# A graph-attention layer on one core: the keys' stage with its work on x spread per tile

## The chip, the cores and the metric

The kernel runs on one core of one Trainium2 chip. The metric is the device time of one execution in microseconds. Before the change the median of 3 runs is 2405.26 us (2391.13 to 2406.40).

## The reference, cut to what matters

x has 6250 rows (nodes) of 256 features; there are 206,250 edges. The part that the change touches is the layer norm and the keys of the linear attention:

```
xn   = layernorm(x)                                  # per row, eps 1e-5
k    = elu(xn @ Wk.T) + 1
ksum = k.sum(rows);  context = k.T @ v   per head    # v = xn @ Wv.T
x1   = x + gnn(xn) + attention(xn)                   # gnn sums (1+eps)*xn and xn[src] by dst
out  = x1 + lstm_ffn(layernorm(x1))
```

The kernel never forms v here: it sums M = xn.T @ k over all rows and multiplies by Wv later. It also keeps xn twice: split into a high part (low 12 mantissa bits cut away) and a low part, both in SBUF as the operand of the later edge sums, and scaled by 1 + eps in DRAM.

## The kernel before, in words

Rows are handled in 49 tiles of 128 (NT), grouped into ten chunks of five (XT = 5, XCH = 10). Each engine has its own hand-written order, and engines meet at semaphores. Chunks of x are loaded by SyncE into a ring of four buffers, `x_ring` (L289). The keys' stage is one loop over the tiles on each engine:

- TensorE (L512 to L554), iteration i: two transposes of tile i (L519), the two key products of tile i-1 (L529, four MATMUL records a tile, as fp32 takes two passes), then the product M of tile i-2 (L536), which needs k_s of that tile.
- ScalarE (L880 to L911), iteration i: copy of the transposed tile to xnT (L886), exp of k_e of tile i-1 (L890). Beside these, once in five tiles: the square root for the row statistics of the chunk two ahead (L871; it needs another activation table than exp, so each one brings two table loads), the high half of a chunk (L900), the chunk scaled by 1 + eps into `row_out` (L906), and the store of `row_out` to DRAM (L910). Before L906 writes the one buffer `row_out`, ScalarE waits for the store of the chunk before (`row_in`); there the store was issued four tiles earlier.
- VectorE (L1303 to L1347), iteration i: k_s = max(k, 0) + exp of tile i-1 (L1310), min(k, 0) of tile i (L1314). Beside these, once in five tiles: `row_stats` of chunk q+2 (L1156, L1160) at tile 0 of a chunk, `row_cut` (L1179) at tile 1, `row_norm` of chunk q+2 (L1166, L1169) at tile 2. At fixed tiles (3, 4, 6, 8, 9, 13, 18, 24, 28, 29, 33) it also does steps on the edge list, L1204 to L1292, some of 2 to 5 us.
- GpSimd (L435 to L452): the low half of a chunk, x minus the cut x (L445), then for each of its tiles k_acc += k_s (L452).

k_e, k_s and the PSUM bank of the keys are double buffered (t % 2, banks 4 and 5). Ahead of the loop VectorE does statistics and normalisation of chunks 0 and 1 and then clears PSUM bank 6 (L1299), which releases TensorE. After the stage follow the queries (from L564), the edge sums (L637), the second norm and the LSTM.

Of the kernel before, what the change touches and what calls it, by code (L numbers as in the profile page):

```python
# [45 lines left out]
CB = (0, 1, 2, 7)  # L46
MAGIC = float(3 * 2 ** 22)
# [16 lines left out]
def build(nc, a, out):  # L64
# [8 lines left out]
    with ExitStack() as ctx:  # L73
# [106 lines left out]
        k_e = [scr[:, v * D:(v + 1) * D] for v in range(2)]  # L180
        k_s = [scr[:, 512 + v * D:512 + (v + 1) * D] for v in range(2)]
        k_acc = scr[:, 1024:1024 + D]
# [103 lines left out]
        def _(sp):  # L286
# [24 lines left out]
            for q in range(XCH - XR):  # L311
                sp.wait_ge(S["m_mm"], XT * (q + 1))
                sp.wait_ge(S["lo_q"], q + 1)
                sp.wait_ge(S["row_act"], q + 1)
                load_x(q + XR)
# [3 lines left out]
            sp.wait_ge(S["lo_q"], XCH - 2)  # L319
# [4 lines left out]
            sp.wait_ge(S["lo_q"], XCH)  # L324
# [89 lines left out]
        def _(pool):  # L414
# [20 lines left out]
            for q in range(XCH):  # L435
                pool.wait_ge(S["cut_v"], q + 1)
                if q == 2:
                    pool.wait_ge(S["key_ok"], 2)
                    pool.dma_start(key_d, key_all).then_inc(S["key_st"], 16)
                if q == XCH // 2:  # L440
                    pool.wait_ge(S["hist_ps"], 2)
                if q == KEY_CH:
                    pool.wait_ge(S["key_st"], 16)
                h = len(tiles(q))
                pool.tensor_tensor(xhl[:, q * XT:q * XT + h, 1, :], x_ring[q % XR][:, 0:h, :], x_cut.bitcast(F32)[:, 0:h, :],  # L445
                                   ALU.subtract).then_inc(S["lo_q"], 1)
                for t in tiles(q):
                    pool.wait_ge(S["k_v"], t + 1)
                    if t:
                        pool.wait_ge(S["acc_q"], t)  # L450
                    r = rows_of(t)
                    pool.tensor_tensor(k_acc[0:r, :], k_acc[0:r, :], k_s[t % 2][0:r, :], ALU.add).then_inc(S["acc_q"], 1)  # L452
# [46 lines left out]
        def _(pe):  # L499
# [12 lines left out]
            for i in range(NT + 2):  # L512
                if i < NT:
                    t = i
                    pe.wait_ge(S["xn_ok"], t // XT + 1)
# [5 lines left out]
                if 1 <= i <= NT:  # L521
# [4 lines left out]
                    if t >= 2:  # L526
                        pe.wait_ge(S["k_v"], t - 1)
                    for c in range(2):
                        last = mm(psum[0:rows_of(t), 4 + t % 2, 0:D], xnT[:, c, t * P:t * P + rows_of(t)], wkv[:, c, :],  # L529
                                  start=(c == 0), stop=(c == 1))  # L530
                    last.then_inc(S["k_ps"], 1)
                if i >= 2:
                    t = i - 2
                    pe.wait_ge(S["k_v"], t + 1)
                    for c in range(2):
                        last = mm(psum[:, 6, c * D:(c + 1) * D], xr(t)[0:rows_of(t), c * P:(c + 1) * P], k_s[t % 2][0:rows_of(t), :],  # L536
# [324 lines left out]
        def _(act):  # L861
# [13 lines left out]
            row_std(1)  # L875
# [4 lines left out]
            for i in range(NT + 1):  # L880
# [6 lines left out]
                if i >= 1:  # L887
                    t = i - 1
                    act.wait_ge(S["k_min"], t + 1)
                    fn(k_e[t % 2], k_e[t % 2], ACT.Exp).then_inc(S["k_exp"], 1)  # L890
                if i < NT:
                    if i % XT == 0 and q + 2 < XCH:
                        row_std(q + 2)
                    if i % XT == 2:
                        act.wait_ge(S["cut_v"], q + 1)
                        if q == XCH // 2:
                            act.wait_ge(S["hist_ps"], 2)
                        if q == KEY_CH:
                            act.wait_ge(S["key_st"], 16)
                        fn(xhl[:, q * XT:q * XT + len(tiles(q)), 0, :], x_cut.bitcast(F32)[:, 0:len(tiles(q)), :], ACT.Copy).then_inc(S["hi_act"], 1)  # L900
                    if i == tiles(q)[-1]:
                        if q == 0:
                            act.wait_ge(S["eps1_v"], 1)
                        if q:
                            act.wait_ge(S["row_in"], 16 * q)
                        fn(row_out[:, 0:len(tiles(q)), :], x_ring[q % XR][:, 0:len(tiles(q)), :], ACT.Copy, scale=eps1).then_inc(S["row_act"], 1)  # L906
                if i and (i % XT == 0 or i == NT):
                    q = (i - 1) // XT
                    act.wait_ge(S["row_act"], q + 1)
                    act.dma_start(row_d[(q * XT + 1) * P:(tiles(q)[-1] + 2) * P, :].rearrange("(t p) d -> p t d", p=P),  # L910
                                  row_out[:, 0:len(tiles(q)), :]).then_inc(S["row_in"], 16)  # L911

            act.wait_ge(S["lo_q"], XCH)
# [224 lines left out]
        def _(dve):  # L1138
# [14 lines left out]
            def row_stats(q):  # L1153
                dve.wait_ge(ld_x[q % XR], 16 * (q // XR + 1) + (16 if q == XCH - 1 else 0))
                for t in range(len(tiles(q))):
                    last = dve.bn_stats(stats[:, 6 * t:6 * t + 6], x_ring[q % XR][:, t, :])  # L1156
                last.then_inc(S["ln_v"], 1)
                dve.wait_ge(S["ln_v"], 2 * q + 1)
                for t in range(len(tiles(q))):
                    last = dve.bn_aggr(mv[q % 2][:, 2 * t:2 * t + 2], stats[:, 6 * t:6 * t + 6])  # L1160
                last.then_inc(S["ln_v"], 1)
                dve.wait_ge(S["ln_v"], 2 * q + 2)

            def row_norm(q):
# [535 lines left out]
```

## Time and profile before

| | us |
|---|---|
| median of 3 runs | 2405.26 |
| lowest, highest | 2391.13, 2406.40 |
| the profiled execution | 2404.46 |
| its span in the profile | 2402.6 |
| keys' stage: first transpose (L519) to the end of the last M product (L536) | 23.5 to 211.6 |
| granted TensorE clock, mean of the span | 0.957 |

Rows of the timeline give start, duration, engine, line, operation and tiles; the bracket is the idle time of that engine just before it, and what ended it. L12 is line 12. PEld is the weight load of TensorE. A granted clock of 1.00 is 2.4 GHz, 0.50 is 1.2 GHz. Tile numbers: `scr` holds k_e, k_s, k_acc and x_cut; `halves` is the split x; `rs_buf` holds `row_out` and one ring buffer, `wx` the other three.

### The profile page before, as it was taken

What the parts mean: (1) busy time and instruction counts of PE and PEld (TensorE: products, weight loads), DVE (VectorE), ACT (ScalarE), POOL (GpSimd) and SP (SyncE); (2) the same over time, 40 slices, a digit from 0 to 9 for tenths busy, and PEclk for the clock granted to TensorE, in tenths of its full rate; (3) what the DMA queues carried; (4) which work ended last, traced back from release to release, by engine and by line L of the source; (5) the groups of instructions that cost most, each with busy time, mean ns of one, the idle gap of its engine ahead of it and who ended that gap; (6) DMA issues with size and microseconds to landing.
All of it is one profiled execution on the core that took longest, in us unless ns stands there. A gap on an engine that the chain in (4) does not pass through costs nothing.

```text
span 2402.6 us, 46078 instructions
## 1 busy us (share of the span) xinstructions
PE 2094.8 (87%) x14220; PEld 1687.2 (70%) x14220; DVE 1617.1 (67%) x4262; ACT 1177.4 (49%) x3155; POOL 160.3 (7%) x185
## 2 busy tenths in 40 slices
PE   4678989999999999999899899988888888888734
PEld 3457876666666666666687788878877887888623
DVE  6756888777777777777277677755565565655684
ACT  2354435555555555555232566655554554555615
POOL 3233001000000000000000000000000000000060
PEclk9789998999999999999999999999999999999975
DMA  4222220010010110100332122233333332334103
GB/s 111 72 75 70 95 96 26 26 31 24 29 31 24 31 31 22 31 28 26 110 97 65 52 119 103 119 103 118 112 94 102 113 117 85 111 111 119 60 7 100
DMA packets 100568, 173.79 MB, mean 72 GB/s; under 512 B 7901, under 2 KB 74779, under 8 KB 100221
## 3 DMA queue, kind: packets, MB, share of 16 engines
q1 hardware_dynamic: 70538, 86.80, 11.3%
q10 hardware_dynamic: 28240, 81.21, 10.9%
q0 software_dynamic: 1744, 5.21, 0.7%
q8 instruction: 24, 0.39, 0.1%
q14 instruction: 22, 0.18, 0.0%
HBM read 114.63 MB, written 58.56 MB: 72 GB/s over the span
## 4 chain that ended last, share of the span: by engine, by line
PE 51%; DVE 18%; ACT 9%; issue 8%; ACTq 2%; DMA 2%; DVEq 1%; POOL 0%; SPq 0%; POOLq 0%
PE psum L626 25%; PE psum L779 8%; PE psum L621 7%; PE psum L736 4%; DVE scr L1579 3%; DVE scr L1577 3%; ACT scr L1047 2%; ACT scr L1055 2%; DVE scr L1575 2%; DMA out_dram<-wq 2%; DVE scr L1371 2%; DVE bufB L1497 1%; DVE bufB L1581 1%; ACTq L1066 1%; ACT scr L1014 1%
## 5 line engine op out<-in xcount | busy, mean ns | idle before, releaser
L626 PE MATMUL psum<-halves,counts 128*128 128x512 f32 x2401 | 759.8, 423 | 16.2 <-ACT counts L952 16.2
L1396 DVE TENSOR_TENSOR wx<-rs_buf 128x392 bf16<-128x392 bf16 (+1 forms) x1568 | 545.0, 390 | 212.2 <-PE psum L621 208.4
L779 PE MATMUL psum<-bufB,wx 128*128 x4800 | 602.0, 282 | 81.8 <-DVE bufB L1581 72.8
L779 PEld LDWEIGHTS psum<-bufB,wx 128*128 128x128 f32 x4800 | 563.7, 193 | 120.0 <-issue 109.1
L952 ACT ACTIVATE counts<-psum 128x392 fp32r<-128x392 f32 x784 | 390.3, 498 | 359.1 <-PE psum L621 357.7
L626 PEld LDWEIGHTS psum<-halves,counts 128*128 128x128 f32 x2401 | 393.7, 189 | 65.9 <-ACT counts L952 21.8
L621 PEld LDWEIGHTS psum<-wx 128*128 128x128 bf16 x3136 | 170.8, 99 | 199.0 <-issue 192.0
L621 PE MATMUL psum<-wx 128*128 128x98 bf16 x3136 | 284.8, 213 | 4.0 <-DVE wx L1396 2.9
L1581 DVE TENSOR_TENSOR bufB<-scr 128x125 f32 (+1 forms) x300 | 87.1, 290 | 146.6 <-ACT scr L1055 146.6
L736 PE MATMUL psum<-bufA,wx 128*128 (+1 forms) x800 | 180.1, 376 | 3.1 <-POOL rs_buf L487 3.1
L1055 ACT ACTIVATE scr<-scr 128x125 f32<-128x125 f32 x300 | 92.2, 307 | 172.1 <-DVE scr L1579 172.1
L736 PEld LDWEIGHTS psum<-bufA,wx 128*128 128x128 f32 x800 | 146.7, 188 | 20.1 <-issue 3.3
L1575 DVE TENSOR_TENSOR scr<-scr 128x125 f32<-128x125 f32 x300 | 85.7, 286 | 106.8 <-ACT scr L1047 106.8
L1014 ACT ACTIVATE scr<-psum,bias_c 128x125 f32<-128x125 f32 x400 | 107.9, 382 | 64.0 <-PE psum L746 63.9
L1042 ACT ACTIVATE psum<-bufA 128x500 f32<-128x500 f32 x144 | 85.7, 595 | 102.1 <-ACT scr L1055 102.1
L1047 ACT ACTIVATE scr<-psum 128x250 f32<-128x250 f32 x300 | 110.2, 367 | 31.8 <-PE psum L779 31.8
L1569 DVE COPY psum<-bufA 128x500 f32<-128x500 f32 x144 | 97.7, 678 | 15.1 <-issue 15.0
L493 POOL TENSOR_TENSOR bufC<-bufC,bufB 128x250 f32<-128x250 f32 x50 | 40.7, 857 | 945.2 <-ACT bufB L1111 945.2
L1497 DVE TENSOR_SCALAR bufB<-psum,bias_c 128x250 f32<-128x250 f32 x192 | 89.0, 474 | 18.0 <-PE psum L736 16.6
L1579 DVE TENSOR_TENSOR scr<-scr 128x125 f32<-128x125 f32 x300 | 87.0, 290 | 10.4
L1577 DVE TENSOR_TENSOR scr<-scr 128x125 f32<-128x125 f32 x300 | 84.8, 283 | 0.0
L1051 ACT ACTIVATE scr<-psum 128x125 f32<-128x125 f32 x300 | 83.4, 278 | 0.0
(249 smaller groups left out, 2232.9 us busy)
## 6 DMA issues: line engine op xcount, KB each, us to landing
bufA<-gates_of_x ACTq DMA_DIRECT2D x144, 500.0 KB, 3.4
gates_of_x<-bufB SPq DMA_DIRECT2D x24, 1000.0 KB, 3.9
x_times_eps_plus_sums<-scr SPq DMA_DIRECT2D x50, 128.0 KB, 1.7
sums_by_feature<-scr SPq DMA_DIRECT2D x50, 128.0 KB, 1.9
scr<-x_times_eps_plus_sums SPq DMA_DIRECT2D x49, 128.0 KB, 2.0
wx<-in_x_dram SPq DMA_DIRECT2D x25, 250.0 KB
x_plus_mix<-wx SPq DMA_DIRECT2D x25, 250.0 KB, 4.7
bufB<-x_plus_mix SPq DMA_DIRECT2D x25, 250.0 KB, 2.7
```

Of the source, the lines that this page charges most:

```text
L621: last = mm(psum[:, CB[u % 4], g * KEYS:(g + 1) * KEYS], oh_l[r][:, g // 2, :, g % 2], oh_m[r][:, g // 2, :, g % 2], start=True, stop=True)
L626: return mm(psum[:, 3 + v, :], cnt[v][:, hi, :], xhl[:, hi, :, :].rearrange("p s d -> p (s d)"), start=(hi == 0), stop=(hi == NT - 1))
L736: last = mm(psum[:, 4 * v + g, c0 * HC:(c0 + 1) * HC].rearrange("p (s j) -> p s j", s=2), wihv[:, k, m * P:(m + 1) * P], ls_in[:, ds(2 * p ...
L779: return mm(gate_half(u, m, gate), whhv[:, k, (2 * gate + m) * P:(2 * gate + m + 1) * P], h, start=False, stop=(k == 1), skip_group_check= ...
L952: fn(cnt[v][:, :, c * u:c * (u + 1)], psum[:, CB[u % 4], 0:PER * KEYS].rearrange("p (c h) -> p h c", h=NT), ACT.Copy).then_inc(S["c_sb"], 1)
L1014: last = fn(to[:, c * CH:(c + 1) * CH], psum[:, 4 * v + g, c * HC + s * CH:c * HC + (s + 1) * CH], function, bias=bias_c[:, 2 * g + c:2 * ...
L1047: fn(half(s_if, m), psum[:, 4 * u + 2 + m, 0:HC].rearrange("p (g j) -> p g j", g=2), ACT.Sigmoid).then_inc(S["hif_act"], 1)
L1055: fn(th[:, m * CH:(m + 1) * CH], tg_c[1 - u][:, 1, m * CH:(m + 1) * CH], ACT.Tanh).then_inc(S["hth_act"], 1)
L1396: last = tt(to, tab2[:, 0:k_, :].unsqueeze(1).broadcast_to([P, PER // 2, k_, 2]), keysT[v][:, part_, g0:g0 + PER // 2, :].unsqueeze(2).bro ...
L1575: tt(prod[:, 1, cut], s_if[:, 1, cut], tg_c[u][:, 1, cut], ALU.mult)
L1577: tt(prod[:, 0, cut], s_if[:, 0, cut], tg_c[u][:, 0, cut], ALU.mult).then_inc(S["prod_v"], 1)
L1579: tt(tg_c[1 - u][:, 1, cut], prod[:, 0, cut], prod[:, 1, cut], ALU.add).then_inc(S["hc_v"], 1)
```

## The change

The work on x is done per tile. ScalarE's iteration i now does, after exp of tile i-1: the high half of that tile, the scaled row copy of that tile, and after the last tile of a chunk the store; the square root of the next chunk follows at the second tile of each chunk. GpSimd does the low half of one tile and then its k_acc step. VectorE cuts one tile per iteration, takes statistics of one tile per iteration of the chunk after the next (the five aggregations together at its end), and normalises the next chunk in its iterations 2, 3 and 4 (two, two and one tile). Ahead of the loop only chunk 0 is done; the statistics of chunk 1 are done inside iteration 0, after `small_vectors`, which moved there from iteration 3. k_e, k_s and the PSUM bank become three each (banks 4, 5, 7), and TensorE's M product lags by three tiles. `row_out` remains one buffer; its wait now stands at the first tile of each chunk, one tile after the store of the chunk before.

```diff
+KB = (4, 5, 7)
-        k_e = [scr[:, v * D:(v + 1) * D] for v in range(2)]
+        k_e = [scr[:, v * D:(v + 1) * D] for v in range(3)]
...
@@ GpSimd @@
-                pool.tensor_tensor(xhl[:, q * XT:q * XT + h, 1, :], x_ring[q % XR][:, 0:h, :], x_cut.bitcast(F32)[:, 0:h, :],
+                pool.tensor_tensor(xhl[:, t, 1, :], x_ring[q % XR][:, j, :], x_cut.bitcast(F32)[:, j, :],
                                    ALU.subtract).then_inc(S["lo_q"], 1)
...
@@ TensorE @@
-                    if t >= 2:
-                        pe.wait_ge(S["k_v"], t - 1)
+                    if t >= 3:
+                        pe.wait_ge(S["k_v"], t - 2)
...
-                if i >= 2:
-                    t = i - 2
+                if i >= 3:
+                    t = i - 3
                     pe.wait_ge(S["k_v"], t + 1)
...
@@ ScalarE @@
             row_std(0)
-            row_std(1)
...
+                    fn(k_e[t % 3], k_e[t % 3], ACT.Exp).then_inc(S["k_exp"], 1)
+                    q, j = t // XT, t % XT
+                    act.wait_ge(S["cut_v"], t + 1)
...
+                    fn(xhl[:, t, 0, :], x_cut.bitcast(F32)[:, j, :], ACT.Copy).then_inc(S["hi_act"], 1)
+                    if t == 0:
+                        act.wait_ge(S["eps1_v"], 1)
+                    if j == 0 and q:
+                        act.wait_ge(S["row_in"], 16 * q)
+                    fn(row_out[:, j, :], x_ring[q % XR][:, j, :], ACT.Copy, scale=eps1).then_inc(S["row_act"], 1)
+                    if t == tiles(q)[-1]:
+                        act.wait_ge(S["row_act"], t + 1)
+                        act.dma_start(row_d[(q * XT + 1) * P:(t + 2) * P, :].rearrange("(t p) d -> p t d", p=P),
+                                      row_out[:, 0:j + 1, :]).then_inc(S["row_in"], 16)
+                if i % XT == 1 and i // XT + 1 < XCH:
+                    row_std(i // XT + 1)
...
@@ VectorE @@
-            row_stats(0)
-            row_norm(0)
-            row_stats(1)
-            row_norm(1)
+            for j in range(XT):
+                row_stats(0, j)
+            for j in range(XT):
+                row_norm(0, j)
...
-                    if t >= 2:
-                        dve.wait_ge(S["m_mm"], t - 1)
-                        dve.wait_ge(S["acc_q"], t - 1)
+                    if t >= 3:
+                        dve.wait_ge(S["m_mm"], t - 2)
+                        dve.wait_ge(S["acc_q"], t - 2)
...
+                    ts(k_e[t % 3], psum[:, KB[t % 3], 0:D], 0.0, None, ALU.min).then_inc(S["k_min"], 1)
+                    row_cut(t)
+                    q, j = t // XT + 1, t % XT
+                    if t == 0:
+                        small_vectors()
+                        for j_ in range(XT):
+                            row_stats(1, j_)
+                    if j >= 2 and q < XCH:
+                        for j_ in ((0, 1), (2, 3), (4,))[j - 2]:
+                            if j_ < len(tiles(q)):
+                                row_norm(q, j_)
+                    q, j = (t - 1) // XT + 2, (t - 1) % XT
+                    if t and q < XCH and j < len(tiles(q)):
+                        row_stats(q, j)
```

## Rows read from the trace of the kernel before

**Rows 1.** Busy time by engine over the keys' stage, with granted clock
```profile
23.40:211.60 188.20, 131.80 (x562) 100.76 (x563) 118.06 (x279) 82.79 (x141) 66.18 (x60) 0.87 0.20 67
```

**Rows 2.** Waits of VectorE, 20 to 215 us: total, times, longest
```profile
DVE scr L1314 <- PE psum L529: 36.5, 26, 3.1
DVE scr L1310 <- issue: 18.7, 7, 2.7
...
DVE scr L1310 <- POOL scr L452: 4.5, 2, 2.6
```

**Rows 3.** Timeline of one group of five tiles, 163 to 180 us
```profile
163.26 0.42 DVE L1310 SCALAR_TENSOR_TENSOR scr<-psum,scr 128x256 f32<-128x256 f32 x1 [2.67 <-issue]
163.60 0.41 DVE L1314 TENSOR_SCALAR scr<-psum 128x256 f32<-128x256 f32 x1
163.93 0.81 DVE L1179 TENSOR_SCALAR scr<-wx 128x1280 int32<-128x1280 int32 x1
...
178.00 1.28 ACT L890 ACT_TABLE_LOAD   x1
...
179.80 0.42 DVE L1310 SCALAR_TENSOR_TENSOR scr<-psum,scr 128x256 f32<-128x256 f32 x1 [2.67 <-issue]
```

**Rows 4.** Timeline, TensorE weight loads of two transposes in a row, full clock
```profile
191.38 0.36 PEld L519 LDWEIGHTS psum<-ident,wx 128*128 128x128 f32 x2
...
193.33 0.35 PEld L519 LDWEIGHTS psum<-ident,wx 128*128 128x128 f32 x2
```

**Rows 5.** Timeline, TensorE after a long idle time
```profile
97.45 2.08 PE L536 MATMUL psum<-scr,wx 128*128 128x256 f32 x4 [4.94 <-DVE scr L1310]
```

**Rows 6.** Start of the stage: VectorE's timeline, and a DMA issue (KB, us to landing)
```profile
18.23 1.74 DVE L1156 BATCH_NORM_STATS2 stats<-wx 128x6 f32<-128x256 f32 x5 [4.99 <-DMA wx<-in_x_dram]
20.00 0.45 DVE L1160 BATCH_NORM_AGGREGATE mv<-stats 128x2 f32<-128x6 f32 x5
...
33.20 0.42 DVE L1310 SCALAR_TENSOR_TENSOR scr<-psum,scr 128x256 f32<-128x256 f32 x1
lin_c<-in_L_ffn_W_lin_dram POOLq DMA_DIRECT2D x1, 2.0 KB, 8.3
```

**Rows 7.** Timeline, the last k_s of the stage on VectorE
```profile
209.98 0.42 DVE L1310 SCALAR_TENSOR_TENSOR scr<-psum,scr 128x256 f32<-128x256 f32 x1 [0.48 <-ACT scr L890]
```

**Rows 8.** Timeline, first and last instruction of the edge steps on VectorE
```profile
40.29 1.22 DVE L1204 CAST bufB<-bufB 101x2049 f32<-101x2049 int32 x1
...
170.98 0.58 DVE L1200 TENSOR_TENSOR bias_c<-bias_c,bias 128x8 f32<-128x8 f32 x1
```

**Rows 9.** Timelines of VectorE and GpSimd: the same work alone and beside the other
```profile
21.11 1.71 DVE L1169 TENSOR_SCALAR wx<-wx,mv,rstd 128x256 f32<-128x256 f32 x5
...
86.88 3.02 DVE L1169 TENSOR_SCALAR wx<-wx,mv,rstd 128x256 f32<-128x256 f32 x5
87.19 1.60 POOL L452 TENSOR_TENSOR scr<-scr 128x256 f32<-128x256 f32 x2
...
98.21 0.42 DVE L1310 SCALAR_TENSOR_TENSOR scr<-psum,scr 128x256 f32<-128x256 f32 x1 [0.48 <-ACT scr L890]
98.71 0.72 POOL L452 TENSOR_TENSOR scr<-scr 128x256 f32<-128x256 f32 x1 [0.51 <-DVE scr L1310]
```

**Rows 10.** Two lines of VectorE over the stage: ns min/median/max
```profile
L1169 DVE TENSOR_SCALAR wx<-wx,mv,rstd x34: 399/404/1349, 21.1 to 185.9; 128x256 f32<-128x256 f32 x34
...
L1156 DVE BATCH_NORM_STATS2 stats<-wx x29: 407/409/418, 27.1 to 176.3; 128x6 f32<-128x256 f32 x29
```

**Rows 11.** ScalarE and GpSimd over the stage, by line: busy us, mean ns, idle before
```profile
L890 ACT ACTIVATE scr<-scr 128x256 f32<-128x256 f32 x49 | 20.4, 417 | 61.3 <-DVE scr L1314 61.0
...
L900 ACT ACTIVATE halves<-scr 128x1280 fp32r<-128x1280 f32 (+1 forms) x10 | 12.5, 1250 | 3.0 <-DVE scr L1179 3.0
...
L452 POOL TENSOR_TENSOR scr<-scr 128x256 f32<-128x256 f32 (+1 forms) x49 | 36.7, 748 | 56.7 <-DVE scr L1310 54.8
```

**Rows 12.** The ten stores of row_out (L910): us from issue to landing
```profile
DMA to landing us min/median/max: 2.9/4.3/6.9
```

More of the change, by code:

```diff
@@ L178, in build @@
         pcol_i = scr[:, P + NGB:P + NGB + 1].bitcast(I32)
-        k_e = [scr[:, v * D:(v + 1) * D] for v in range(2)]
-        k_s = [scr[:, 512 + v * D:512 + (v + 1) * D] for v in range(2)]
-        k_acc = scr[:, 1024:1024 + D]
+        k_e = [scr[:, v * D:(v + 1) * D] for v in range(3)]
+        k_s = [scr[:, (3 + v) * D:(4 + v) * D] for v in range(3)]
+        k_acc = scr[:, 6 * D:7 * D]
         x_cut = scr[:, 1792:1792 + XT * D].bitcast(I32).rearrange("p (t d) -> p t d", d=D)
@@ L434, in _ @@
             pool.wait_ge(S["acc_z"], 1)
[L435 to L437 removed]
+            for t in range(NT):
+                q, j = t // XT, t % XT
+                pool.wait_ge(S["cut_v"], t + 1)
+                if j == 0 and q == 2:
                     pool.wait_ge(S["key_ok"], 2)
                     pool.dma_start(key_d, key_all).then_inc(S["key_st"], 16)
[L440 removed]
+                if j == 0 and q == XCH // 2:
                     pool.wait_ge(S["hist_ps"], 2)
[L442 removed]
+                if j == 0 and q == KEY_CH:
                     pool.wait_ge(S["key_st"], 16)
[L444 to L445 removed]
+                pool.tensor_tensor(xhl[:, t, 1, :], x_ring[q % XR][:, j, :], x_cut.bitcast(F32)[:, j, :],
                                    ALU.subtract).then_inc(S["lo_q"], 1)
[L447 to L452, printed above, removed]
+                pool.wait_ge(S["k_v"], t + 1)
+                if t:
+                    pool.wait_ge(S["acc_q"], t)
+                r = rows_of(t)
+                pool.tensor_tensor(k_acc[0:r, :], k_acc[0:r, :], k_s[t % 3][0:r, :], ALU.add).then_inc(S["acc_q"], 1)
             pool.wait_ge(S["key_st"], 16)
@@ L511, in _ @@
             pe.wait_ge(S["m_z"], 1)
-            for i in range(NT + 2):
+            for i in range(NT + 3):
                 if i < NT:
                     t = i
-                    pe.wait_ge(S["xn_ok"], t // XT + 1)
+                    pe.wait_ge(S["xn_ok"], t + 1)
                     if t >= 2:
@@ L907, in _ @@
[L907 to L913, printed above, removed]
+                    fn(k_e[t % 3], k_e[t % 3], ACT.Exp).then_inc(S["k_exp"], 1)
+                    q, j = t // XT, t % XT
@@ L1151, in _ @@
             dve.memset(inv_d[:, :], 1.0 / D)
[L1153 to L1162, printed above, removed]
@@ L1164, in row_norm @@
-            def row_norm(q):
-                dve.wait_ge(S["ln_std"], q + 1)
-                dve.reciprocal(rstd[q % 2][:, 0:len(tiles(q))], rstd[q % 2][:, 0:len(tiles(q))]).then_inc(S["ln_r"], 1)
-                dve.wait_ge(S["ln_r"], q + 1)
-                for t in range(len(tiles(q))):
-                    last = ts(x_ring[q % XR][:, t, :], x_ring[q % XR][:, t, :], mv[q % 2][:, 2 * t:2 * t + 1],
-                              rstd[q % 2][:, t:t + 1], ALU.subtract, ALU.mult)
-                last.then_inc(S["xn_ok"], 1)
@@ L1173, in row_cut, with row_stats @@
-            def row_cut(q):
-                dve.wait_ge(S["xn_ok"], q + 1)
-                if q:
-                    dve.wait_ge(S["hi_act"], q)
-                    dve.wait_ge(S["lo_q"], q)
-                ts(x_cut[:, 0:len(tiles(q)), :], x_ring[q % XR][:, 0:len(tiles(q)), :].bitcast(I32), -4096, None, ALU.bitwise_and).then_inc(S["cut_v"], 1)
+            def row_stats(q, j):
+                if j == 0:
+                    dve.wait_ge(ld_x[q % XR], 16 * (q // XR + 1) + (16 if q == XCH - 1 else 0))
+                    if q:
+                        dve.wait_ge(S["ln_v"], 2 * q)
+                last = dve.bn_stats(stats[:, 6 * j:6 * j + 6], x_ring[q % XR][:, j, :])
+                if j == len(tiles(q)) - 1:
+                    last.then_inc(S["ln_v"], 1)
+                    dve.wait_ge(S["ln_v"], 2 * q + 1)
+                    for t in range(len(tiles(q))):
+                        last = dve.bn_aggr(mv[q % 2][:, 2 * t:2 * t + 2], stats[:, 6 * t:6 * t + 6])
+                    last.then_inc(S["ln_v"], 1)
```

61 lines of the change are left out of this document (27 added, 34 removed).

## The prediction

> **What bounds the kernel now.** I read the busy times of the keys' stage first [rows 1]: in 188.2 us no engine is full (TensorE 131.8, VectorE 118.1, ScalarE 82.8, GpSimd 66.2), and the TensorE clock is granted at 0.87. So order and waiting bound it. The waits of VectorE say which [rows 2]: 36.5 us for the keys' product of TensorE, 18.7 us for an exp that came late, 4.5 us for GpSimd. The timeline of one five-tile group shows it from inside [rows 3]: from one late exp to the next (163.26 to 179.80) it takes 16.5 us, and each time VectorE waits 2.67 us, behind a table reload of 1.28 us. Where nothing disturbs, a tile takes TensorE 1.95 us, from transpose to transpose [rows 4], or 9.7 us for five; after a long idle time four M matmuls take 2.08 us [rows 5], the clock then being at its lower level, 1.2 GHz. So 16.5 us a group stand against 9.7, and the loss is in the bursts on VectorE, ScalarE and GpSimd.
>
> **The sum's frame.** I count on VectorE's k_s instructions, since each waits for everything. Before: k_s of tile 1 at 33.20 [rows 6], of tile 35 at 179.80 [rows 3], of tile 48 at 209.98 [rows 7]. Between the first two are 34 tiles, 6.8 groups; at 16.5 us these are 112.2 of the 146.6 us, and the other 34.4 us are the edge steps (38 instructions between the two of [rows 8]). The last 13 tiles take 30.2 us.
>
> **Start: 8.4 us gained.** Now the loop waits for nothing of chunk 1, and iteration 0 holds it. x of chunk 1 lands at 18.23; the last small vector is issued by GpSimd near 11.1 and takes 8.3 us [rows 6], so it lands at 19.4. Small vectors (0.8 in the timeline), statistics 1.74 and aggregation 0.45 [rows 6] end near 22.4; square root, copy, table reload and exp (0.3 + 0.4 + 1.28 + 0.42) put k_s of tile 1 at 24.8, against 33.20. The reload is one more than before, as a tenth square root stands between two exps; it is in this sum.
>
> **VectorE's own work in a group.** k_s, min and cut start 0.33 us apart [rows 3]. One cut of 256 columns is a fifth of 0.81 us at least, 0.33 at most; I take 0.22. So 0.88 us a tile, 4.4 a group. Five norms 1.71 [rows 9] and a reciprocal 0.1; five statistics 1.74 and aggregation 0.45 [rows 6]: 8.4 us in all. VectorE's added waits (its own norm, cuts of five tiles before) are for work long done.
>
> **GpSimd beside it: +3.2 us a group.** GpSimd's k_acc starts 0.50 us after k_s and takes 0.73 [rows 9], thus until 1.23; the per-tile cut starts at 0.66, in its middle. A low half of 256 columns will take about as long as a k_acc, 0.73, and follows at once, beside the norms. Five norms beside two k_acc take 3.02 us instead of 1.71 [rows 9], and a single one up to 1349 ns instead of 404, while the statistics never differ (407 to 418) [rows 10]. If the cut waits for the end of k_acc it costs 0.5 us more a tile, 2.5 a group, and the norms some 0.7 more: 3.2. Lower end 0 (the phases miss each other), upper end 4.8 (cut and norms, 2.8 us alone, at 2.7 times their length, the pace of the norms while GpSimd ran). I take 3.2, so 11.6 us: iterations of 2.2, 1.7, 2.9, 2.7 and 2.1 us. GpSimd itself has 10 x 0.73 = 7.3 us plus waits: no bound, and its bursts, 4.5 us of waits [rows 2], go.
> The Trainium skill (SBUF — State Buffer, Who interferes with whom) says that VectorE and GpSimd take a shared port pair as an exclusive lock for a whole instruction, so that the loser blocks fully. The 1349 ns agree. By that rule each small cut pays up to a whole k_acc, and splitting multiplies the meetings; by the mere pace of the norms it would be 3.0 instead of 3.2.
>
> **ScalarE: a new wait.** Its work rises: a high half of five tiles is 1250 ns, an exp of one 417 [rows 11]; at 0.33 us from start to start, five tiles of four instructions take 6.6 us, with two reloads and the square root 9.5. That fits in 11.6, as ScalarE idles 61.3 us before the exps now [rows 11]. But the order is bad. Lay k_s of tile 5q-1 at 0. The store of the old chunk is issued at -0.4, right behind the row copy of tile 5q-1. The row copy of tile 5q could start at 1.7, but waits for that store to land: 2.9 to 6.9 us, median 4.3 [rows 12], where it used to have four tiles' time. Before, both the store and a load of x followed the end of a chunk; the load now comes some two tiles later, so I take 3.8, between the least and the median: landing at 3.4. Behind it in ScalarE's queue stand row copy 0.35, reload 1.28, square root 0.30, copy 0.33, reload 1.28 and exp 0.42: k_s of tile 5q+1 at 7.4, where VectorE was ready at 3.9. This is 3.5 us of waiting, against 2.67 before. Ends: 2.6 (landing 2.9) and 6.6 (6.9).
>
> **TensorE.** The third buffer and bank give it one tile, 1.95 us, before M stalls, so a keys' product is ready when VectorE comes back from a long step; most of the 36.5 us should go, being replaced by VectorE's own longer iterations. TensorE still starves in each ScalarE burst (about 3 us, the next transposed tile is copied behind it), and at the lower clock its next products come late: 0 to 2.2 us a group, I take 0.7. So a group is 11.6 + 3.5 + 0.7 = 15.8 us against 16.5: 0.7 x 6.8 = 4.8 us gained.
>
> **Edge steps: 6.1 us gained.** They are VectorE's own work and stay: the 34.4 us, and some 0.6 because a GpSimd step now stands beside each. But ScalarE's burst goes on beneath the one at tile 6 (3.4 us saved) and the store lands beneath those at 4, 9, 24 and 29 (3.3 us together). 35 - 6.7 = 28.3 against 34.4.
>
> **Tail: 5.9 us lost.** Statistics and norms of the last chunk used to be over at tile 37 and now reach to tile 44. Tiles 36 to 39 with their wait 13.0; tiles 40 to 44 without statistics 9.4 + 3.5; the last four at TensorE's 1.95 with one store wait of 1.5: 9.3; late products 0.9. Together 36.1 against 30.2.
>
> **Other edits.** The extra scratch, the changed SyncE counts and three PSUM banks cost nothing: x loads have over ten us to be used, SyncE waits behind them only. If that cover failed, statistics would wait for x; a load takes some 4 to 5 us, so even two tiles later it is in time. The 640 KB store stays one DMA.
>
> **Sum.** 8.4 + 4.8 + 6.1 - 5.9 = 13.4 us. The profiled execution took 2404.46 us (span 2402.6 and 1.9 around it), so 2391; it lies 0.8 under the median of the runs. All later stages follow unchanged.
>
> **Rivals.**
> A, GpSimd's meetings cost nothing: a group is ScalarE's chain to 7.4 plus three iterations of 5.5, 12.9 us, and 3.6 x 6.8 = 24.5 us are gained there; the tail loses 1.5: 2404.5 - 8.4 - 24.5 - 6.1 + 1.5 = 2367. For it: GpSimd has only 7.3 us of work a group. Against it: cut and k_acc hang on the same k_s.
> B, the single row buffer decides, slower than before: the store lands in 5.3 us, ScalarE's chain grows by 1.5, TensorE starves for 5 us in each group and its next tiles run at 1.2 GHz (+2.2 instead of 0.7). A group is 18.8: 2.3 x 6.8 = 15.6 lost, the tail 13 lost, 14.5 gained at start and edges: 2404.5 + 14 = 2418. It decides from a landing of some 4.8 us on. For it: half of the stores before took 4.3 us or more [rows 12]. Against it: a load of x no longer falls beside the store.
> C, a wash: cut and norms pay the upper end, 1.6 us more a group: 2391 + 11 + 3 = 2405. The third buffer then does not shorten anything.
>
> **Chances.** Forecast 0.50 (own range 2381 to 2400), A 0.27, B 0.12, C 0.11. About 1%, 24 us, is what a measurement of this kernel can tell from no change. Faster by more: 0.23 of A and 0.07 of the forecast, 0.30; slower by more 0.06; within it 0.64. The range 2368 to 2415 leaves out the better half of A and the worse half of B.
>
> **What would show it.** k_s of tile 1 near 25 us; ScalarE's row copy of the first tile of each chunk idle before it, ended by the store's DMA; VectorE waiting some 3.5 us for an exp once a group; cuts of about 0.6 to 0.8 us instead of 0.3 and norms with a median well over 404 ns (alone: A); VectorE's waits for L529 well under 36.5 us; the last k_s near 196.6. Wrong if ScalarE shows no wait at the store, or if the granted clock of the stage falls under 0.8 (B).

## The result and the profile after

The changed kernel takes 2377.03 us (median of 4 runs, 2367.57 to 2377.68) against 2403.77 (median of 4 runs, 2391.13 to 2406.40) of the kernel before: ratio 0.9888, 95% interval [0.9862, 0.9915]. The forecast was a gain of 13.4 us; it is 26.7, twice as much. The profiled execution took 2377.68 us, its span is 2375.9 (before 2404.46 and 2402.6).

First, where the 26.7 us of span lie. Three lines of the window view of the changed kernel: the keys' stage, the stretch from its end to the edge sums, and the LSTM sweeps (columns: busy time of TensorE, its weight loads, VectorE, ScalarE, GpSimd, each with its count; granted clock; DMA share; GB/s).

```profile
14.00:192.10 178.10, 134.21 (x562) 103.01 (x563) 136.22 (x333) 100.18 (x224) 73.53 (x99) 0.83 0.26 77
192.10:338.90 146.80, 135.04 (x719) 117.51 (x718) 119.28 (x102) 60.93 (x127) 3.57 (x6) 1.00 0.31 98
1552.00:2236.00 684.00, 603.15 (x4804) 564.60 (x4804) 408.04 (x1366) 373.07 (x1348) 0.00 (x0) 0.98 0.35 108
```

The kernel before, same two later stretches:

```profile
211.60:360.00 148.40, 136.66 (x719) 118.75 (x718) 119.28 (x102) 60.93 (x127) 3.57 (x6) 0.99 0.29 94
1573.00:2263.00 690.00, 602.41 (x4804) 563.86 (x4804) 408.20 (x1370) 373.12 (x1349) 0.00 (x0) 0.99 0.35 107
```

Against [rows 1] VectorE and ScalarE are busier and the stage still ends earlier; TensorE's clock in it fell from 0.87 to 0.83. The last k_s moved from 209.98 [rows 7] to 190.51, so 19.5 us are won in the stage. Between there and the edge sums another 1.6 us is won: TensorE is busy for 135.04 us there instead of 136.66 with the same instructions, at a granted clock of 1.00 instead of 0.99. And 5.7 us come from a stage that the change does not touch, the sweep matmuls of line L779: the first line is of the kernel before, the second of the changed one.

```profile
L779 PE MATMUL psum<-bufB,wx x4800: 274/275/572, 1573.6 to 2262.4; 128*128 x192
```
```profile
L779 PE MATMUL psum<-bufB,wx x4800: 274/275/572, 1552.5 to 2235.6; 128*128 x192
```

They run for 688.8 and for 683.1 us, with the same matmuls. In six profiles of the kernel before, five of them with empty waits added behind the stage (The sweeps, below), the last k_s stands between 206.2 and 210.3; in three of the changed kernel between 189.3 and 190.5. The 19.5 thus belong to this pair of profiles; other pairs would give 16 to 21. Counted from the k_s of tile 1 to that of tile 48, VectorE's idle time falls from 62.3 to 32.1 us, while its own work, from start to start without the waits, grows from 114.5 to 131.9. The change buys 30 us of waiting with 17 us of work, most of it the cuts.

The waits of the changed kernel in its stage, which answer to [rows 2] (us in total, times, longest):

```profile
DVE scr L1310 <- ACT scr L889: 26.6, 11, 4.4
ACT rs_buf L901 <- DMA x_times_eps_plus_sums<-rs_buf: 11.2, 7, 2.2
DVE scr L1314 <- PE psum L529: 8.2, 10, 2.9
DVE stats L1155 <- DMA wx<-in_x_dram: 3.1, 1, 3.1
```

VectorE's waits for the keys' product fell from 36.5 to 8.2 us [rows 2]. Its waits for an exp were 18.7 us of [rows 2] and this line of the same view,

```profile
DVE scr L1310 <- ACT scr L890: 7.9, 13, 2.4
```

together 26.6; they stayed at 26.6, and there is a new wait of ScalarE for the store of `row_out`. The timeline from 153 to 160 us shows both, and answers to [rows 3]:

```profile
153.37 0.39 DVE L1310 SCALAR_TENSOR_TENSOR scr<-psum,scr 128x256 f32<-128x256 f32 x1
...
155.30 0.51 ACT L901 ACTIVATE rs_buf<-rs_buf,cols 128x256 f32<-128x256 f32 x1 [2.21 <-DMA x_times_eps_plus_sums<-rs_buf]
155.82 1.28 ACT L871 ACT_TABLE_LOAD   x1
157.12 0.30 ACT L871 ACTIVATE rstd<-mv,eps_ln 128x5 f32<-128x5 f32 x1
157.33 0.36 ACT L885 ACTIVATE bufC<-psum 128x256 f32<-128x256 f32 x1
157.71 1.28 ACT L889 ACT_TABLE_LOAD   x1
...
159.00 0.42 ACT L889 ACTIVATE scr<-scr 128x256 f32<-128x256 f32 x1
...
159.45 0.42 DVE L1310 SCALAR_TENSOR_TENSOR scr<-psum,scr 128x256 f32<-128x256 f32 x1 [4.40 <-ACT scr L889]
```

The row copy of the first tile of a chunk waits for the store of the chunk before; behind it stand a table load, the square root, the copy, another table load and the exp, and VectorE waits 4.40 us.

The cuts of VectorE over the stage (ns min/median/max; 39 of the 49, the other ten read the ring buffer in `rs_buf`), and one of them beside GpSimd:

```profile
L1179 DVE TENSOR_SCALAR scr<-wx x39: 281/704/1116, 17.7 to 189.9; 128x256 int32<-128x256 int32 x39
```
```profile
147.06 0.73 POOL L452 TENSOR_TENSOR scr<-scr 128x256 f32<-128x256 f32 x1 [1.21 <-DVE scr L1310]
```
```profile
147.24 0.70 DVE L1179 TENSOR_SCALAR scr<-wx 128x256 int32<-128x256 int32 x1
```

A cut alone takes 281 ns; most take 704. The one shown begins while k_acc runs and ends 0.15 us behind it. All 49 together are busy for 31.2 us; the 41 that take longer than 0.45 us all overlap a k_acc in time.

### The profile page after: what moved, and what is told of

The parts are those of the page before. It is cut to its first block, busy times and chain, and to the rows that moved or that the text cites. A ratio compares the mean times of both kernels' runs of the same rounds, so it can differ in the third digit from the quotient of the medians.

```text
span 2375.9 us, 46270 instructions
## 1 busy us (share of the span) xinstructions
PE 2098.5 (88%) x14220; PEld 1689.3 (71%) x14220; DVE 1632.7 (69%) x4301; ACT 1195.0 (50%) x3237; POOL 166.1 (7%) x224
## 3 DMA queue, kind: packets, MB, share of 16 engines
q1 hardware_dynamic: 70538, 86.80, 11.4%
## 4 chain that ended last, share of the span: by engine, by line
PE 53%; DVE 21%; ACT 10%; issue 8%; DMA 4%; ACTq 2%; DVEq 1%; POOL 0%; SPq 0%; POOLq 0%
PE psum L626 26%; PE psum L779 8%; PE psum L621 7%; PE psum L736 4%; DVE scr L1584 3%; DVE scr L1582 3%; ACT scr L1043 2%; ACT scr L1051 2%; DMA out_dram<-wq 2%; DVE scr L1580 2%; DVE scr L1376 2%; DVE bufB L1502 1%; DVE bufB L1586 1%; ACTq L1062 1%; ACT scr L1010 1%
## 5 line engine op out<-in xcount | busy, mean ns | idle before, releaser
L626 PE MATMUL psum<-halves,counts 128*128 128x512 f32 x2401 | 759.8, 423 | 16.2 <-ACT counts L948 16.2
L779 PE MATMUL psum<-bufB,wx 128*128 x4800 | 602.8, 283 | 75.1 <-DVE bufB L1586 66.2
L779 PEld LDWEIGHTS psum<-bufB,wx 128*128 128x128 f32 x4800 | 564.4, 193 | 113.4 <-issue 102.5
L1051 ACT ACTIVATE scr<-scr 128x125 f32<-128x125 f32 x300 | 92.2, 307 | 172.1 <-DVE scr L1584 172.1
L1038 ACT ACTIVATE psum<-bufA 128x500 f32<-128x500 f32 x144 | 85.7, 595 | 95.5 <-ACT scr L1051 95.4
L1043 ACT ACTIVATE scr<-psum 128x250 f32<-128x250 f32 x300 | 110.2, 367 | 32.4 <-PE psum L779 32.3
L529 PE MATMUL psum<-wk,bufC 128*128 128x256 f32 (+1 forms) x196 | 66.2, 470 | 25.7 <-ACT bufC L885 25.3
```

Source lines behind the costliest of these rows:

```text
L626: return mm(psum[:, 3 + v, :], cnt[v][:, hi, :], xhl[:, hi, :, :].rearrange("p s d -> p (s d)"), start=(hi == 0), stop=(hi == NT - 1))
L779: return mm(gate_half(u, m, gate), whhv[:, k, (2 * gate + m) * P:(2 * gate + m + 1) * P], h, start=False, stop=(k == 1), skip_group_check= ...
L1043: fn(half(s_if, m), psum[:, 4 * u + 2 + m, 0:HC].rearrange("p (g j) -> p g j", g=2), ACT.Sigmoid).then_inc(S["hif_act"], 1)
L1051: fn(th[:, m * CH:(m + 1) * CH], tg_c[1 - u][:, 1, m * CH:(m + 1) * CH], ACT.Tanh).then_inc(S["hth_act"], 1)
```

## The experiments

The edits are against the changed kernel, except where the kernel before is named. "Last k_s" is where the last L1310 of the stage starts; it is 190.51 in the changed kernel. The runs of the kernel before beside each experiment are those of the same chip.

### The third buffer, taken away and alone

```diff
-KB = (4, 5, 7)
+KB = (4, 5)
...
-                    if t >= 3:
-                        pe.wait_ge(S["k_v"], t - 2)
+                    if t >= 2:
+                        pe.wait_ge(S["k_v"], t - 1)
```

> The changed kernel with two buffers of k_e and k_s, two banks and M lagging by two tiles, as before; all else per tile. Theory S (the third buffer carries the gain, because TensorE's waits for k_s went from 39.4 to 16.7 us and VectorE's for the product from 36.5 to 8.2): most of the gain is lost, 2393 us or more, VectorE waits for L529 over 25 us. Theory P (spreading the work per tile, and GpSimd's and ScalarE's bursts with it, carries it; the third buffer only covers ScalarE's reload): 2378 to 2384, waits for L529 under 18 us.

The other way round, three of k_e, k_s and PSUM banks, and TensorE's lag of three tiles, in the kernel before:

> The kernel before with nothing but the third buffer and bank and M lagging by three. Theory S: 2383 to 2390 against 2404, VectorE's waits for L529 fall from 36.5 to under 12 us. Theory P: 2396 to 2404, as the bursts of five (statistics, norms, GpSimd's 2.9 us) still stand in the same places; the waits for L529 fall, but come back as VectorE waiting for exp.

Without the third buffer, with the spreading alone, the changed kernel takes 2380.56 us beside 2402.34, ratio 0.9914 [0.9898, 0.9931], last k_s 192.88. The third buffer alone gives 2389.99, ratio 0.9944 [0.9924, 0.9963], last k_s 194.00. So each theory fails once: the first run is in the range of P and the second in that of S, though the waits for L529 miss both limits. Their waits of VectorE for the keys' product, first with the spreading alone, then with the third buffer alone:

```profile
DVE scr L1314 <- PE psum L529: 20.8, 22, 2.4
```
```profile
DVE scr L1315 <- PE psum L530: 17.5, 19, 2.9
```

From 209.98, the third buffer alone moves the last k_s by 16.0 us, the spreading alone by 17.1, both by 19.5. Each by itself takes away about half of the 36.5 us of waits for TensorE, together they take away 28; what they leave is ScalarE's exp, 21.3 us of waits with the spreading alone, 28.5 with the third buffer alone, 26.6 with both. In the stage they are substitutes: beside the spreading the third buffer is worth 2.4 us, not 16.

The loop without its start says more. From the k_s of tile 1 to that of tile 48 the kernel before takes 176.8 us, the spreading alone 168.0, the third buffer alone 162.3, both 164.0 (163.2 and 163.4 in two more profiles). Inside the loop the third buffer alone is as good as both, or 1 to 2 us better: VectorE's own work is 121.0 us there against 131.9, since its cuts stay in one instruction a chunk. What the spreading adds beside the third buffer is the earlier start, 26.46 against 31.75 for the k_s of tile 1. Of the 16.0 us of the third buffer alone, 12.4 reach the total; behind its stage the stretch to the edge sums takes 2.4 us longer, at a granted clock of 0.98.

### ScalarE's chain: the store, and the square root

The store of a chunk in two pieces, each with a semaphore of its own, so that the first tile of the next chunk waits only for the piece of the first three tiles, issued two tiles before the other piece, and the fourth tile for the other piece:

```diff
+                    if j == 3 and q:
+                        act.wait_ge(S["pad_v"], 2 + 16 * q)
...
-                    if t == tiles(q)[-1]:
+                    if j == 2 or t == tiles(q)[-1]:
+                        j0 = 0 if j == 2 else 3
                         act.wait_ge(S["row_act"], t + 1)
...
-                                      row_out[:, 0:j + 1, :]).then_inc(S["row_in"], 16)
+                                      row_out[:, j0:j + 1, :]).then_inc(S["row_in" if j == 2 else "pad_v"], 16)
```

> The changed kernel with each chunk's store in two, tiles 0 to 2 after the third and the rest after the last, so that a row copy waits for a store issued at least two tiles earlier. If the wait for the one row buffer is on the path (11.2 us before L901, up to 2.2 each, in front of both table reloads): VectorE's waits for exp fall from 4.4 to some 2.5 us a group, 2377 becomes 2366 to 2369, last k_s near 181. If it is hidden by VectorE's own work: within 2 us of 2377. Ten more DMA issues on ScalarE with a wait for its own write, 0.5 each, may give back up to 4 us.

2364.08 us beside 2402.34, ratio 0.9847 [0.9830, 0.9863]: 13.0 us better than the changed kernel, a little more than expected; the last k_s is at 177.19. ScalarE's waits for the store are gone, and VectorE's for the exp fell from 26.6, longest 4.4, to

```profile
DVE scr L1315 <- ACT scr L891: 15.9, 11, 2.8
```

What is left, up to 2.8 us, is close to the 2.67 of [rows 3], which stood behind a table load; the next run takes the table loads away.

In the next run the square root of the row statistics is left out (an Identity stands in its place, which needs no other table), so that rows are scaled wrongly but nothing else changes:

> The changed kernel with ScalarE's square root replaced by identity, which needs no other table: leaves out the square root of the row statistics, and with it both table reloads a chunk (20 x 1.28 us). If these stand in the chain before the exp once a group: VectorE's waits for exp fall from 26.6 to under 8 us, and the last k_s from 190.5 to 172 to 176, the time to 2359 to 2363. If VectorE's own work and the GpSimd meetings bind: last k_s above 182.

```profile
DVE scr L1310 <- ACT scr L889: 9.5, 9, 1.8
ACT rs_buf L901 <- DMA x_times_eps_plus_sums<-rs_buf: 11.0, 7, 2.0
```

2359.93 us beside 2402.11, ratio 0.9821 [0.9804, 0.9837]. The time and the last k_s, 172.33, are where they were expected if the table loads stand in the chain; the waits for the exp are a little over it. The wait at the store is still there, 11.0 us, and yet the waits for the exp fell by 17.1 us and the time by 17.1. The Trainium skill (ScalarE: Activation LUTs, Table sets: the hidden batching unit) wants activation calls batched by table set, and the same page (What ACT_TABLE_LOAD costs) prices one switch at 1283 ns and a drain of about 1380 ns; the load agrees (1.28 us), a drain does not show, since the square root starts at 157.12, 0.02 us behind the end of a load that began at 155.82.

### GpSimd beside VectorE

Statistics ahead of the cut, so that the cut no longer falls into k_acc:

```diff
+                    q, j = (t - 1) // XT + 2, (t - 1) % XT
+                    if t and q < XCH and j < len(tiles(q)):
+                        row_stats(q, j)
                     row_cut(t)
...
-                    q, j = (t - 1) // XT + 2, (t - 1) % XT
-                    if t and q < XCH and j < len(tiles(q)):
-                        row_stats(q, j)
```

> The changed kernel with VectorE's statistics of the tile placed ahead of its cut instead of behind it; same instructions. If the cut's 0.70 us (0.28 alone) is waiting for the end of GpSimd's k_acc: the cut's median falls to 0.35 to 0.45 us, and 3 of 5 iterations get 0.3 us shorter: 5 to 9 us, 2368 to 2372. If the 0.70 us are the cut's own length at 256 columns: its median stays near 0.70 and the time at 2377. Rival: hi and low halves start 0.35 us later and ScalarE's chain with them, then 2375 to 2379 with the cut at 0.4.

GpSimd's sum over the keys cut to 2 of its 256 columns (the sum over the keys is left out but for these; its steps stay where they are):

> The changed kernel with GpSimd's k_acc step on 2 of its 256 columns: leaves out most of the sum of keys (the accumulator starts at 64 instead, so that later values keep their size). If the cut waits for k_acc to end: its median falls from 0.70 to about 0.3 us, a group gets 1.2 to 1.5 us shorter where VectorE binds (three of five iterations): 2363 to 2370. If the meeting only moves on to the low half and the norms: cut at 0.3, norms longer, 2374 or more.

The cuts of the two on the same 39 tiles, in this order:

```profile
L1179 DVE TENSOR_SCALAR scr<-wx x39: 258/366/1567, 17.2 to 184.3; 128x256 int32<-128x256 int32 x39
```
```profile
L1179 DVE TENSOR_SCALAR scr<-wx x39: 275/283/452, 16.4 to 179.1; 128x256 int32<-128x256 int32 x39
```

The first takes 2372.63 us, ratio 0.9882 [0.9865, 0.9898], last k_s 184.85; the second 2368.19, ratio 0.9857 [0.9839, 0.9875], last k_s 179.71. With hardly any k_acc a cut is down at 283 ns: the 704 are the meeting. Over all 49 tiles the cuts' busy time falls from 31.2 us to 19.3 in the first and 14.0 in the second. In the first the last k_s shows only 5.7 of these 11.9 us: the waits for the exp rose from 26.6 to 30.0 us and those for the keys' product from 8.2 to 9.9. Eight cuts still meet a k_acc, one of them behind a low half besides (1567 ns). In the second VectorE's own work from tile 1 to 48 falls by 16.4 us, and longer waits take 6.6 of them back; its four times spread from 2363.56 to 2371.31, so its 8.8 us are good to a few us.

### Both together, and the square root besides

> The changed kernel with both: the store in two, and the statistics ahead of the cut. If ScalarE's chain of store wait and two reloads hid part of what the shorter cuts save, the two add up to more than their sum alone (2364.1 and 2372.6 against 2377.0, so 17.4 us): 2356 to 2359. If both shorten the same idle time of VectorE, it stays within 2 us of the split alone, 2362 to 2366.

2361.08 us beside 2402.11, ratio 0.9825 [0.9809, 0.9841]; last k_s

```profile
174.54 0.42 DVE L1315 SCALAR_TENSOR_TENSOR scr<-psum,scr 128x256 f32<-128x256 f32 x1 [0.28 <-ACT scr L891]
```

This is the fastest kernel here that computes everything, 16 us under the changed one. The edits were worth 13.0 and 4.4 alone and are worth 16.0 together, so they add up but for 1.4 us; the time lies between the two ranges that were expected.

> The changed kernel with the store in two, the statistics ahead of the cut, and identity in place of the square root: leaves out the square root and both table reloads a chunk. Alone against 2377 the store in two gave 13, the order 4.4, the missing reloads 17.1 us, and store and order together 15.9. If all shorten one chain (ScalarE's from exp to exp), the three together end where TensorE's 1.95 us a tile and VectorE's own work bind: 2352 to 2356, groups of 10.5 to 11.5 us. If they are separate costs they add to 33 us: 2344.

Without the square root as well: 2348.89 us beside 2399.64, ratio 0.9779 [0.9747, 0.9812]; waits for the exp 3.0 us, for the keys' product 13.8. That is 28 us under the changed kernel, where 16.0 and 17.1 would add up to 33: between the two expectations. That the two pieces of ScalarE's chain overlap in part, and that each also delays something of its own, fits this but is not shown.

### The start

Statistics of chunk 1 back ahead of the loop:

> The changed kernel with the statistics of chunk 1 done ahead of the loop again, as before (its normalisation stays in the loop). The loop then starts when chunk 1 has landed, some 8 us later. If the start carries the 6.7 us seen at k_s of tile 1 (26.46 against 33.20): 2382 to 2385. If x of chunk 2, for which VectorE now waits 3.1 us, bounds the start in any case: 2378 to 2380.

2378.47 us beside 2402.11, ratio 0.9907 [0.9891, 0.9924], k_s of tile 1 at 27.90 instead of 26.46, last k_s 190.82 instead of 190.51: the second of the two expectations. Moving these statistics is worth 1.4 us where it stands and 0.3 at the end of the stage; in ten profiles with the changed start the k_s of tile 1 stands between 24.85 and 26.94, so the 1.4 is hardly more than the scatter. The rest of the start's 6.7 us comes with what else no longer stands ahead of iteration 1 (norms and square root of chunk 1, high half and row copies of five tiles at once); these were not tried one by one.

### The sweeps

Identical code ran 5.7 us faster in the changed kernel. What differs in it is how many instructions stand ahead of the loop in each engine's program. So instructions that wait for a semaphore long at its value, and so do nothing, were put behind the keys' stage: 82 in ScalarE's program, as many as the profile page counts more in the changed kernel (3237 against 3155), and 72 in VectorE's, as many as its trace holds more there (39 that work and 33 that wait). The edit for 82 writes 164 waits; the trace shows 82 instructions for them.

```diff
+            for _ in range(164):
+                act.wait_ge(S["k_min"], NT)
             act.wait_ge(S["lo_q"], XCH)
```

> The kernel before with 82 instructions more in ScalarE's program ahead of the last M product's end (waits on a count long reached), as many as the change added; nothing else. The LSTM's sweeps (L779) took 688.8 us before and 688.7 in the kernel before with a third buffer, but 683.1 in the changed kernel and in every variant of it, though that code is the same. If this hangs on where ScalarE's loop lies in its program: about 683 us here. If not, 688.7 stays.

> The kernel before with 72 instructions more in VectorE's program ahead of the sums of the keys (waits on a count long reached), as many as the change added; nothing else. If the sweeps' 5.7 us hang on where VectorE's loop lies in its program: L779 takes about 683 us here. If they hang on ScalarE's or on neither: 688.7.

The sweep matmuls with the 82 on ScalarE, then with the 72 on VectorE:

```profile
L779 PE MATMUL psum<-bufB,wx x4800: 275/275/572, 1573.3 to 2256.3; 128*128 x192
```
```profile
L779 PE MATMUL psum<-bufB,wx x4800: 274/275/572, 1580.9 to 2271.0; 128*128 x192
```

683.0 us with ScalarE's program shifted, 690.1 with VectorE's. The first execution took 2398.54 us and its span is 2396.7, 5.9 under that of the kernel before; its sweeps account for 5.8 of them. The second took 2412.89; its edge sums start 6.7 us later, since the 72 empty instructions hold VectorE from 210.28 to 217.50, about 0.1 us each, ahead of the queries. The 128 on ScalarE, below, have such a price too: 153.8 us from the last k_s to the edge sums instead of 150.0.

Then whether it is the place of the loop or the mere shift, and whether the changed kernel can lose the gain:

> The kernel before with 32 waits on k_min, already satisfied, in ScalarE's program behind the keys' stage (16 instructions): a shift of 16 instead of 82. If any shift helps, or the number of instructions ahead of the loop only matters past one bound that lies low, the sweeps take 683 us as with 82. If the gain hangs on where the loop lies against some boundary, 16 may well not reach it: 688.8 us as before. Nothing else moves; total 2399 or 2404 accordingly.

> The same with 48 instructions. Place against a boundary: 683 or 688.8 us, and together with 16, 82 and 128 it tells from where to where the gain lasts. Mere shift: 683.

> The same with 128 instructions. If the place counts and repeats with a period that divides 128 instructions, the sweeps are back at 688.8 us; if a bound was passed for good between 0 and 82, they take 683.

> The changed kernel with 92 satisfied waits in ScalarE's program behind the keys' stage (46 instructions), which together with its own 82 are 128. If the sweeps' 5.7 us are the place of ScalarE's loop and nothing else of the change, the sweeps here take what they take in the kernel before with 128 added: both 683 or both 688.8. If the gain came from something else in the changed kernel, it stays at 683 whatever the other does.

| instructions ahead of ScalarE's loop, beyond the kernel before | kernel | L779, first to last, us |
|---|---|---|
| 0 | before | 688.8 |
| 16 | before | 688.8 |
| 48 | before | 683.5 |
| 82 | before | 683.0 |
| 82 | changed | 683.1 |
| 128 | before | 688.1 |
| 128 | changed | 688.2 |

The line of the last one:

```profile
L779 PE MATMUL psum<-bufB,wx x4800: 274/275/572, 1551.9 to 2240.1; 128*128 x192
```

The two kernels follow one curve. It falls between 16 and 48 and is up again at 128. The variants above fill it in: they have 63 (no square root), 73 and 92 (store in two, without and with the square root) instructions more there and take 682.9 to 683.6. So the 5.7 us are the place of ScalarE's loop and nothing that the change does to the data or the order. This rests on the spans of L779 and not on the times, since these are single executions and the kernel before alone ranges over 15 us; they took 2399.41, 2399.11, 2403.05 and 2382.12 us (the last is the changed kernel with 46, 5.1 over its median).

### The changed kernel again

> The changed kernel itself once more, beside the others on one chip: 2375 to 2379, with L779 in 683 us and the last k_s at 190 to 191, if both differences belong to the kernel; if they were chance, one of them moves by 3 us or more.

2376.88 us beside 2399.64, ratio 0.9905 [0.9878, 0.9931], waits for the exp 26.7 us, last k_s 189.32: on another chip the same kernel within 0.2 us, and the kernel before 4 us faster than in the first comparison. Ratios here carry about that much.

## Why the prediction was wrong, point by point

The direction and the frame were right: no engine bound, order and waiting did. The size was half of the truth. Two steps failed: the time from tile 1 to tile 35, put 8.8 us too long in its waits, its own work and its edge steps, and "All later stages follow unchanged", where 7.3 us were won. The forecast put the last k_s at 196.6; it is at 190.51, 6.1 us earlier; start and tail erred the other way and hide 2.7 of the 8.8. The rest of the missing 13.3, 7.3 us, lies behind the stage.

**Start: 8.4 forecast, 6.7 measured.** k_s of tile 1 came at 26.46, not 24.8. The step that failed is "x loads have over ten us to be used": that does not hold for chunk 2. The forecast took 4 to 5 us for a load; this one is issued at 7.9 us, among the first loads, and lands at 26.1 (26.7 in the kernel before), and VectorE waited for it in iteration 1:

```profile
26.12 0.43 DVE L1155 BATCH_NORM_STATS2 stats<-wx 128x6 f32<-128x256 f32 x1 [3.05 <-DMA wx<-in_x_dram]
```

**Group of five: 15.8 forecast; 15.3, 16.2, 15.8 and 15.9 measured** (from k_s of tile 21 to that of tile 41). Two of its three terms held. VectorE's own work was put at 11.6: in 143.67 to 159.45 it is 15.8 less the wait of 4.4, or 11.4. The cuts were forecast at 0.22 + 0.5 us and are 0.70. The wait for the exp was put at 3.5, with ends 2.6 and 6.6; its five between tile 1 and 35 are 1.67, 3.54, 3.54, 3.68 and 2.70, the two behind them 4.40 and 4.38. The third term, 0.7 for late products of TensorE, is not there: from tile 21 to 36 VectorE waits for none; edge steps of 2.5 us in these tiles fill its place. The norms cost what was forecast (a group's five start over 2.5 us, 1.7 alone), but their median, 403 ns, did not rise as foretold: 20 of the 49 took longer, up to 834. The factor 2.7 behind the upper end of 4.8 stands in none of the rows (3.02 against 1.71 us is 1.8, 1349 against 404 ns is 3.3). The store, taken to land in 3.8 us, lands in

```profile
x_times_eps_plus_sums<-rs_buf ACTq DMA_DIRECT2D x9, 640.0 KB, 3.3
```

3.3: the load of x indeed no longer falls beside it.

**Tiles 1 to 35: this is what was mis-sized, the edge steps the most.** From tile 1 to tile 35 the forecast has 135.7 us (15.8 x 6.8 and 28.3), measured are 126.9 (26.46 to 153.37). Laid out by VectorE's time: waits for the exp 17.1 forecast, 15.1 measured; waits for the keys' product 4.8 (0.7 x 6.8) and 2.5; its own work with the edge steps 113.9 and 109.3. So each of three parts was too high. By line, the third is 76.9 us for keys and x, where 78.9 (11.6 x 6.8) were forecast, and 32.3 for the edge steps, where 35.0 were. "They are VectorE's own work and stay" is what failed: by the same count they take 37.1 us in the kernel before, and 4.8 of these went. 0.7 are the small vectors, which moved ahead of tile 1; most of the rest is meetings that the edge steps had held with GpSimd's long low half, which the change cuts into fifths. Before, GpSimd, then VectorE:

```profile
54.70 3.80 POOL L445 TENSOR_TENSOR halves<-wx,scr 128x1280 fp32r<-128x1280 f32 x1 [6.63 <-DVE scr L1179]
```
```profile
55.79 3.79 DVE L1218 TENSOR_SCALAR bufB<-bufB 101x2048 f32<-101x2048 f32 x1
59.62 1.63 DVE L1220 TENSOR_SCALAR bufB<-bufB 101x2048 f32<-101x2048 f32 x1
```

and VectorE after:

```profile
45.23 1.23 DVE L1218 TENSOR_SCALAR bufB<-bufB 101x2048 f32<-101x2048 f32 x1
46.49 1.23 DVE L1220 TENSOR_SCALAR bufB<-bufB 101x2048 f32<-101x2048 f32 x1
```

2.56 and 0.40 us. The forecast said that splitting multiplies the meetings, and priced that; it did not look for the long meetings that splitting ends. This agrees with the rule of the Trainium skill that it quoted (SBUF — State Buffer, Who interferes with whom), that the loser is blocked for the other's whole instruction: GpSimd's step is over at 58.50, and VectorE's, 1.23 us alone, ends at 59.58, 1.08 behind it. So a long GpSimd instruction is the dear one. Of the two waits, long edge steps hide both the exp (the burst behind tile 6 is wholly beneath one) and TensorE's lateness; the forecast hid only the first.

**Tail: 36.1 forecast, 37.1 measured** (153.37 to 190.51), against 30.2 before: statistics and norms reach later, as worked out.

**"All later stages follow unchanged" failed.** 5.7 us of the sweeps are the place of ScalarE's loop (shown by the padded kernels), 1.6 us lie between the last k_s and the edge sums. These go with TensorE's clock. The stretch takes 148.3 or 148.4 us in every profile where its granted clock is 1.00, and the kernel before with 16 empty instructions is one of them; where the clock is 0.99 it takes 150.0 or more. In the kernel before it is granted at 0.66 from 225 to 230 us, in the changed kernel at 1.00 there. Of the eleven profiles of the changed kernel and its variants ten have the short stretch, of the seven of the kernel before one. So the 1.6 us are TensorE's clock and not work saved; whether the change favours the clock there was not tried.

**The rivals.** A, GpSimd's meetings free, gave 2367 and is nearly as far off as the forecast, on the other side, and false: the cuts take 704 ns, and without k_acc 283, which is worth 8.8 us. Even then the groups take 14.1 to 16.2 us, not the 12.9 of A, as the waits for the exp stay. C, the upper end, did not come: the third buffer does shorten something, 2.4 us. B, the single row buffer decides and makes it slower, did not come either, as the store lands in 3.3 us where B needs 4.8, and the stage's clock, 0.83, stays over 0.8. But its mechanism is real: 13.0 us are lost at that one buffer. It was priced in the forecast's 3.5 us stall, which came true; the gain of the change is what remains beside it.

Sum: 13.4 forecast, -1.7 start, +8.8 tiles 1 to 35, -1.0 tail (19.5 in the stage), +1.6 and +5.7 behind it: 26.8, measured 26.7.

## What to carry to other kernels

When a long instruction of GpSimd is cut into pieces, price both sides: the meetings with VectorE that are added (0.4 us a tile here) and the long ones that end (3.79 us for 1.23 us of work). Buffering deeper and spreading bursts attack the same waits, so try each alone before paying for both: here the third buffer alone gave a loop as short as both together, and the spreading beside it only an earlier start. And look next at the in-order queue that neither touches: here a store's wait and two table loads ahead of an exp, worth 13 and 17 us. And compare the stages that a change leaves alone: 5.7 of 26.7 us came from where a loop lies in its engine's program, and an edit ahead of it can lose them, as 46 added instructions did.

## What the runs showed of the hardware that was not expected

ScalarE's turn from the last gate of one step (L1055 before, L1051 after) to the DMA issue of the next, at two places of the sweeps. The kernel before:

```profile
1705.60 0.31 ACT L1055 ACTIVATE scr<-scr 128x125 f32<-128x125 f32 x1 [0.61 <-DVE scr L1579]
1706.28 0.34 ACTq L1066 DMA_DIRECT2D bufA<-gates_of_x  x1
1706.88 0.59 ACT L1042 ACTIVATE psum<-bufA 128x500 f32<-128x500 f32 x1 [0.98 <-ACT scr L1055]
```

The changed kernel:

```profile
1700.93 0.31 ACT L1051 ACTIVATE scr<-scr 128x125 f32<-128x125 f32 x1 [0.61 <-DVE scr L1584]
1701.51 0.34 ACTq L1062 DMA_DIRECT2D bufA<-gates_of_x  x1
1702.11 0.60 ACT L1038 ACTIVATE psum<-bufA 128x500 f32<-128x500 f32 x1 [0.88 <-ACT scr L1051]
```

0.68 us before and 0.58 after, in every other of the 144 turns (in the others both kernels wait 0.49); over the sweeps this line's idle time is 102.1 us before, 95.4 in the changed kernel and 95.4 in the kernel before with 82 instructions on ScalarE. The sweeps' time follows it. With 72 instructions on VectorE the turn is 0.69 us, as before, so the 1.3 us by which those sweeps are longer still come from elsewhere. What makes the turn longer or shorter was not tried; the steps of 16, 48, 82 and 128 instructions only show that it comes and goes with the place.
